# Relu and the product with the sign as single instructions of 1024 columns in a fused Gram, long-convolution and Haar kernel

## The reference

```python
# layer 0: channel attention from the Gram matrix of an image
att = einsum('bcn,bdn->bcd', q, q); rev = max(att) - att
x = gamma * (softmax(rev) @ q) + x
# layers 1 and 3: long convolution by an implicit filter k = hx * hy (outer product), plus bias
y = irfft2(rfft2(x) * rfft2(k))[..., :L, :L];  x = y + x * bias
# layer 2: thresholding in the Haar domain, P = 2 branches
f1 = haar2d(x)
for i in range(P):
    f4 = einsum('bchw,oc->bohw', f1 * v[i], conv_w[i])
    acc = acc + sign(f4) * relu(abs(f4) - tau[i])
x = haar2d(acc, inverse=True) + x
```

## Time and profile before

| | |
|---|---|
| median of 3 runs | 6031.75 us (6027.64 to 6034.47) |
| profiled execution | 6024.16 us, span 6022.3 us |
| mean granted TensorE clock | 0.968 of full speed |
| busy: PE, DVE, ACT, POOL | 5710.0 (95%), 3918.0 (65%), 3794.7 (63%), 2526.9 (42%) us |
| relu (L764) | x896, 556.1 us busy |
| product with the sign (L1135) | x896, 1038.8 us busy |
| GpSimd idle before L1135, for ScalarE's relu | 1815.4 us |

### The profile page before, as it was taken

The page is one execution under the profiler, slowest core; times in us unless marked ns, Lnnn a source line. Parts: engine busy times, 40 slices in busy tenths (PEclk is TensorE's granted clock), DMA queues, the critical chain, the costliest instruction groups (busy, mean ns, idle before and its releaser), DMA issues.

```text
span 6022.3 us, 154233 instructions
## 1 busy us (share of the span) xinstructions
PE 5710.0 (95%) x47200; PEld 4861.0 (81%) x47200; DVE 3918.0 (65%) x6260; ACT 3794.7 (63%) x6105; POOL 2526.9 (42%) x2436
## 2 busy tenths in 40 slices
PE   5897899999999999999999999999999999998689
PEld 3683788888888888888888888888888888897479
DVE  1241687557865678657775577756776578866866
ACT  1333676657766677666775577665776567756855
POOL 0000565225642366324552255423553246634942
PEclk7896999999999999999999999999999999999889
DMA  8778665766657666676666766576666755444234
GB/s 290 240 227 272 205 212 187 244 213 210 212 189 253 202 209 212 202 244 198 210 205 220 226 205 210 184 252 207 213 211 199 249 173 182 158 130 129 73 91 129
DMA packets 770795, 1216.97 MB, mean 202 GB/s; under 512 B 78854, under 2 KB 475047, under 8 KB 770568
## 3 DMA queue, kind: packets, MB, share of 16 engines
q1 hardware_dynamic: 623112, 945.61, 51.7%
q10 hardware_dynamic: 147456, 268.50, 11.8%
HBM read 808.07 MB, written 405.73 MB: 202 GB/s over the span
## 4 chain that ended last, share of the span: by engine, by line
PE 88%; DMA 3%; ACT 2%; DVE 2%; issue 2%; SPq 1%; POOL 1%; ACTq 1%; DVEq 0%; POOLq 0%
PE ps L478 29%; PE ps L480 15%; PE ps L528 9%; PE ps L496 9%; PE ps L504 8%; PE ps L488 7%; PE ps L456 4%; PE ps L538 4%; PE ps L644 3%; DMA mixed<-x 2%; DVE pix L1103 1%; ACT ps L894 1%; DMA mixed<-mid 1%; ACT x L845 1%; DVE ps L1116 0%
## 5 line engine op out<-in xcount | busy, mean ns | idle before, releaser
L1135 POOL TENSOR_TENSOR mag<-mag,sgn 128x512 f32<-128x512 f32 x896 | 1038.8, 1160 | 1815.4 <-ACT mag L764 1815.4
L1152 POOL TENSOR_TENSOR split_a<-field,split_a 128x512 fp32r<-128x512 f32 x512 | 651.0, 1271 | 1635.8 <-ACT split_a L825 1635.8
L478 PE MATMUL ps<-tab_a,img 128*128 128x256 f32 x4096 | 1237.2, 384 | 15.7 <-issue 14.7
L478 PE MATMUL ps<-tab_b,mid 128*128 128x256 f32 x4096 | 1224.6, 381 | 4.4 <-ACT mid L777 4.4
L997 DVE TENSOR_TENSOR held<-ps,v_t 128x1024 f32<-128x1024 f32 x448 | 548.5, 1224 | 619.2 <-PE ps L528 618.8
L480 PEld LDWEIGHTS ps<-tab_a,img 128*128 128x128 f32 x4096 | 782.8, 191 | 107.6
L480 PEld LDWEIGHTS ps<-tab_b,mid 128*128 128x128 f32 x4096 | 778.6, 190 | 105.0
L480 PE MATMUL ps<-tab_a,img 128*128 128x128 f32 x4096 | 790.1, 275 | 0.0
L480 PE MATMUL ps<-tab_b,mid 128*128 128x128 f32 x4096 | 787.0, 274 | 0.0
L758 ACT ACTIVATE sgn<-held 128x1024 bf16<-128x1024 f32 x448 | 473.3, 1056 | 456.5 <-DVE res L1008 454.3
L478 PEld LDWEIGHTS ps<-tab_a,img 128*128 128x128 f32 x4096 | 664.6, 192 | 73.6 <-issue 16.9
(11 more groups left out here) (97 smaller groups left out, 9090.2 us busy)
## 6 DMA issues: line engine op xcount, KB each, us to landing
img<-mixed SPq DMA_DIRECT2D x512, 256.0 KB, 3.2
tab_a<-filt SPq DMA_DIRECT2D x1024, 128.0 KB, 2.8
tab_b<-filt SPq DMA_DIRECT2D x1024, 128.0 KB, 3.0
out<-res SPq DMA_DIRECT2D x512, 256.0 KB, 3.1
coef<-res ACTq DMA_DIRECT2D x496, 256.0 KB, 3.5
pix<-in_x_pix SPq DMA_DIRECT2D x240, 512.0 KB, 4.7
mixed<-x ACTq DMA_DIRECT2D x448, 256.0 KB, 3.5
pix<-in_x_rows SPq DMA_DIRECT2D x128, 512.0 KB, 5.2
```

The lines of the kernel that those rows point to most:

```text
L478: nc.tensor.matmul(o_ps, src[:, 0, H * half:H * half + H], tab[:, N - 1::-1], start=True, stop=False)
L1135: nc.gpsimd.tensor_tensor(mag[:, s], mag[:, s], sgn[:, s], ALU.mult).then_inc(c_mult, 1)
L1152: nc.gpsimd.tensor_tensor(split_a[:, 1], src, split_a[:, 0].bitcast(F32), ALU.subtract)\
```

## The change

Relu of a step becomes one ScalarE instruction over both halves, at the place of the first; it waits for all pair sums of the step before and adds 2 to c_relu, so that the counts of other engines hold. The relu of half 1 behind the mid copy goes. On GpSimd the two products with the sign become one over 1024 columns, which waits for the whole relu and adds 2 to c_mult. The two pair sums stay. The code serves all seven stages of forward and shrinking; `last_shrink` is unchanged.

```diff
-                    def relu(s):
+                    def relu():
                         act.wait_ge(c_less, m + 1 + CR)
-                        act.wait_ge(c_pair, 2 * m + s - 1 + CR)
-                        nc.scalar.activation(mag[:, s], diff[:, s], ACT.Relu).then_inc(c_relu, 1)
+                        act.wait_ge(c_pair, 2 * m + CR)
+                        nc.scalar.activation(mag[:].rearrange("p s n -> p (s n)"),
+                                             diff[:].rearrange("p s n -> p (s n)"), ACT.Relu).then_inc(c_relu, 2)
...
                         sign()
-                        relu(0)
+                        relu()
...
                             first_copy()
-                        relu(1)
...
-                    for s in range(2):
-                        pool.wait_ge(c_relu, 2 * m + s + 1 + CR)
-                        pool.wait_ge(c_sign, m + 1 + CR)
-                        nc.gpsimd.tensor_tensor(mag[:, s], mag[:, s], sgn[:, s], ALU.mult).then_inc(c_mult, 1)
+                    flat = mag[:].rearrange("p s n -> p (s n)")
+                    pool.wait_ge(c_relu, 2 * m + 2 + CR)
+                    pool.wait_ge(c_sign, m + 1 + CR)
+                    nc.gpsimd.tensor_tensor(flat, flat, sgn[:].rearrange("p s n -> p (s n)"), ALU.mult)\
+                        .then_inc(c_mult, 2)
```

## The result

The changed kernel takes 6044.30 us (median of 11 runs, 6034.44 to 6054.00), the kernel before 6029.49 (11 runs, 6026.18 to 6034.47). The ratio is 1.0024, 95% interval 1.0015 to 1.0033: slower by 14.8 us between the medians, forecast 13.2. The profiled execution took 6045.30 us, its span 6043.5.

What follows compares the result with a forecast made beforehand. TensorE was taken to bound the gram stages, the mid-copy chain stage b = 6. There 30 waits of 0.44 us made 13.2 us, all else nothing; added to 6031.75 this gave 6045 us, range 6030 to 6053.

Steps and rivals of the forecast that it cites:

- the chain of the mid copy: Stage b = 6: row products through VectorE and ScalarE to mid, then the first toeplitz product; said to bound that stage already.
- The loop over two steps: Stage b = 6: the mid chain spans two steps, so the delay enters once; 11.54 us grows to 11.98.
- 30 waits: Stage b = 6: first toeplitz products of steps 5, 7, ... 63 wait for mid; 0.44 us each, 13.2 us.
- T to P: Stage b = 6: from a step's first toeplitz product to the next start of row products, 4.18 us.
- P to T: Stage b = 6: row products' start to the toeplitz product that waits on their chain, 7.42 us, forecast 7.8 to 7.9.
- Rival A: Stage b = 6: the loop spans one step, so each of about 60 pays 0.44; 26 us, 6058; chance 0.07.
- The size of the delay: ScalarE: merged relu makes the copies behind it late by 0.44 us, bounds 0.40 and 0.52.
- GpSimd costs nothing: GpSimd: the single product starts after the whole relu, yet pair sums just meet VectorE's field sum; cost nothing.
- Gram stages cost nothing: The 384 steps of the gram stages: the longer relu fits ScalarE's 0.64 us of cover; nothing lost or gained.
- Rival C: ScalarE's queue is what counts: 0.08 us freed per step, res copy earlier in drains; faster, 6026; chance 0.05.
- Rival D: Seventh stage: TensorE's waits also lower its granted clock to 0.98; 7 us more, 6052; chance 0.05.
- Rival B: No change: mid's delay is absorbed, seventh stage stays at 5.77 us a step; 6032, or 6038 in part; chance 0.19.

Runs made afterwards that it cites:

- e9: Changed kernel with the mid copy moved ahead of store, sign and relu, directly behind abs, in all seven stages: 6028.32 us, ratio 0.9997 to the kernel before.
- e3: Kernel before with the whole change only in the stage without Gram products (b = 6): 6042.21 us, ratio 1.0021.
- e4: Kernel before with the whole change only in the six gram stages: 6027.07 us, ratio 0.9998.
- e5: Kernel before, nothing merged, relu of half 1 moved ahead of the split copy and the mid copy: 6044.39 us, ratio 1.0026.
- e7: Changed kernel plus an extra 512-column activation in b = 6, between relu and the split copy: 6060.25 us, ratio 1.0049 to the kernel before.
- e1: Changed kernel with relu merged but GpSimd's two products of 512 columns kept: 6044.62 us, ratio 1.0026 to the kernel before.
- e2: Kernel before with only GpSimd's product merged, waiting for both relu halves: 6056.48 us, ratio 1.0047.
- e6: Changed kernel with the merged relu moved behind the mid copy: 6056.11 us, ratio 1.0045 to the kernel before.
- e8: Changed kernel plus an extra 512-column activation in b = 6, behind the mid copy: 6040.16 us, ratio 1.0020 to the kernel before.

## Why the prediction was right

- *What bounds.* That the seventh stage hung on the chain of the mid copy, though TensorE was busy 334.56 of 334.70 us, held: in e9 the same stage takes 5.67 us a step instead of 5.77. e3 and e4 show that this stage, and it alone, carries the cost.
- *The loop over two steps.* Forecast 11.98 us for two steps, measured 2 x 5.98 = 11.96. With the 4.18 us from T to P, that leaves 7.78 from P to T in the mean (7.8 to 7.9 forecast). e5 and e7 moved mid by another 0.52 us each in their way and the stage answered with 15.1 and 15.2 us, as 30 waits do. Rival A, each step pays, falls with e7.
- *The size of the delay.* Forecast 0.44, measured 0.94 - 0.52 = 0.42 in pitch. 30 x 0.42 = 12.6, and the stage grew by 12.2. The drain adds 0.4 (12.21 us from its last row products to the eight products behind the low piece, 11.85 before), which makes the 12.6. The medians' 14.8 lies 2 above that, within the interval (1.0015 to 1.0033 is 9 to 20 us). The totals can't tell 12.6 from 13.2 or 14.8; the size rests on the traces, and that the medians came so near to the forecast is in part luck. The rule in "ScalarE: Activation LUTs", "What ACT_TABLE_LOAD costs", from the Trainium skill would have made it 0.427 and a duration of 1039 ns for 1024 columns; the trace has 1042. For the saving in ScalarE's busy time the prediction had 0.09 us per step; 31.5 us in 448 steps are 0.07.
- *GpSimd costs nothing.* Right for the change (e1), for the reason given: it got its data early enough. Its margin was thinner than I wrote. I forecast no wait of the field sum for pair_sum; there are 12 in the window, 0.2 us each, one in four steps, where GpSimd starts its pair sums 0.16 us late behind the product. VectorE's idle time before held took them. With the product late by one place more (e2, e6) the same chain and the drains behind it cost 27 us. That the field sum's waits are harmless in the change is borne out by e1, which has two products and is no faster.
- *Gram stages cost nothing.* Right: the wait for L504 went from 0.64 to 0.20 us, forecast 0.2.
- *Rival C* (ScalarE's queue length counts) falls with e8: 512 columns more behind mid, no cost. Nor did the res copy's earlier place in the drain bring a gain: the six gaps between the stages sum to 1916.3 us against 1916.0. *Rival D* (the clock) falls: 1.00 in the stage with a wait in every second step. *Rival B* falls with the interval and with the 5.98 us a step.
- What the forecast didn't ask is how late relu may stand. It asked only what stands behind relu on ScalarE; e2 and e6 show that GpSimd, which waits for it, bounds its place from the other side.

## What to carry to other kernels

An engine that looks full by its busy time can still be waiting, if its records overlap; compare the distance between the same instruction in successive steps with the sum of its own work. Where a wait passes once through a loop that spans two steps, a delay on it costs half per step, and the loop's length (4.18 + 7.4 us here) says how many steps it spans. Before two instructions are merged, ask what stood between them: the copy that frees another engine's bank should not stand behind work that nobody waits for yet, and the cheapest mend here was its place, not the merging.

## What the runs showed of the hardware that I had not expected

GpSimd's product of fp32 with bf16 took 1160 ns for 512 columns and 2136 for 1024, so 976 ns for 512 more columns and 184 ns that are fixed; the merging saves only the fixed part. TensorE's granted clock sets part of what a drain costs. Windows of 10 us from the start of the eight products, in the third drain of the kernel before and of e2 (the columns of the earlier trace rows):

```profile
2442.00:2452.00 10.00, 7.82 (x36) 5.77 (x37) 6.70 (x19) 4.70 (x9) 3.82 (x3) 0.77 0.87 311
2459.57:2469.57 10.00, 7.95 (x32) 6.08 (x32) 5.79 (x16) 3.98 (x7) 3.78 (x3) 0.68 0.81 308
```

In the kernel before, where TensorE had waited 1.62 us for the low piece, such windows of the six gram stages have 1.00, 1.00, 0.77, 0.77, 0.78 and 1.00, and the eight products took 1.13 us in every one. In e2, behind waits of 2.84 to 2.93 us, they have 0.68, 0.67, 0.68, 0.83, 0.83 and 0.68, and the products took 1.13 to 2.07 us. So the clock could fall behind either wait, differently from drain to drain of one execution. In e2 it fell in every drain, and early enough to slow the products in five of the six. A longer wait there cost more than its own length (14.5 us in the six gaps between stages, of which 7.5 are the longer waits); how much of the rest is the clock's is not separated by any run.
